# Attention keys computed fifteen heads ahead of the scores in place of twelve, with two buffers for the mean squares

## The reference

```python
q = (layernorm(x) @ Wq).reshape(B, Sq, H, D)
k = (ctx @ Wk).reshape(B, Skv, H, D)
v = (ctx @ Wv).reshape(B, Skv, H, D)
q = rmsnorm(q, gq)            # x * rsqrt(mean(x^2) + eps) * g
k = rmsnorm(k, gk)
attn = softmax(einsum('bqhd,bkhd->bhqk', q, k) / sqrt(D))
x = x + einsum('bqhk,bkhd->bqhd', attn, v).reshape(B, Sq, H * D) @ Wo
```

## Time and profile before

| | |
|---|---|
| median of 3 runs | 1373.06 us (1372.28 to 1373.51) |
| the profiled execution | 1372.17 us |
| its span, first to last instruction | 1370.4 us |
| PE busy | 1353.0 us, 99% of the span |
| PEld busy | 1214.4 us, 89% |
| DVE busy | 919.3 us, 67% |
| ACT busy | 919.9 us, 67% |
| POOL busy | 539.8 us, 39% |
| DMA | 166.36 MB, mean 121 GB/s |
| mean granted TensorE clock | 0.999 of full speed |

### The profile page before, as it was taken

One profiled execution on the slowest core, in us unless ns is written; L12 is line 12 of the kernel. 1 busy time (PEld: TensorE's weight loads), 2 busy tenths in 40 slices (PEclk: granted clock), 3 DMA queues, 4 the chain that ended last, 5 costly groups with the idle time before them and its releaser, 6 DMA issues. The chain is left out here.

```text
span 1370.4 us, 28300 instructions
## 1 busy us (share of the span) xinstructions
PE 1353.0 (99%) x9496; PEld 1214.4 (89%) x9496; DVE 919.3 (67%) x2414; ACT 919.9 (67%) x2019; POOL 539.8 (39%) x477
## 2 busy tenths in 40 slices
PE   9999999999999999999999999999999999999997
PEld 9889878999999999999999999999888888888885
DVE  6312047667777777777777777766558878887886
ACT  5566668888888878888888888787724443444342
POOL 1044326433323323323332423324824655565551
PEclk9999999999999999999999999999999999999999
DMA  8877723333444444444444444434562353334312
GB/s 248 237 197 222 207 73 95 111 104 120 126 115 130 122 123 116 141 114 115 139 117 121 132 110 129 123 92 141 159 187 62 66 111 64 71 66 113 62 32 44
DMA packets 186403, 166.36 MB, mean 121 GB/s; under 512 B 87938, under 2 KB 155540, under 8 KB 184468
## 3 DMA queue, kind: packets, MB, share of 16 engines
q1 hardware_dynamic: 178980, 151.50, 40.3%
q10 hardware_dynamic: 7280, 13.06, 3.6%
HBM read 124.57 MB, written 33.02 MB: 115 GB/s over the span
## 5 line engine op out<-in xcount | busy, mean ns | idle before, releaser
L816 POOL TENSOR_TENSOR rk_sp<-ms_sp,neg_half 124x6 f32<-124x6 f32 x128 | 170.2, 1353 | 462.7 <-DMA ms_sp<-ms 462.7
L1253 DVE CUSTOM_DVE_ANT_0 sc<-psS,rk 100x361 f32<-100x361 f32 x256 | 136.5, 533 | 131.8 <-PE psS L905 92.6
L1048 ACT ACTIVATE pr<-ex,ri 100x361 f32<-100x361 f32 x256 | 152.6, 596 | 43.4 <-DVE ri L1241 43.4
L1041 ACT ACTIVATE ex<-sc,nb,rq_all 100x361 f32<-100x361 f32 x256 | 174.8, 683 | 4.0 <-DVE nb L1262 3.9
L933 PE MATMUL psZ<-pT_hi,cK_hi 120*128 120x400 f32 (+1 forms) x384 | 132.6, 345 | 0.0
L933 PE MATMUL psZ<-pT_hi,cK_lo 120*128 120x400 f32 (+1 forms) x384 | 132.1, 344 | 0.0
L933 PE MATMUL psZ<-pT_lo,cK_hi 120*128 120x400 f32 (+1 forms) x384 | 131.9, 343 | 0.0
L918 PEld LDWEIGHTS psP<-ident,pr 100*120 100x120 f32 (+1 forms) x768 | 73.6, 138 | 42.6 <-issue 35.3
L1023 ACT ACTIVATE ring_hi<-bank 128x362 fp32r<-128x362 f32 x125 | 59.1, 473 | 75.6 <-PE bank L881 74.7
L1233 DVE TENSOR_TENSOR pT_lo<-psP,pT_hi 122x600 fp32r<-122x600 f32 x128 | 98.9, 773 | 1.2 <-ACT pT_hi L1072 1.1
L905 PE MATMUL psS<-ring_hi,q_hi 128*100 128x362 f32 x256 | 96.8, 378 | 2.0 <-DVE mx L1253 2.0
(11 more groups left out here) (324 smaller groups left out, 3895.5 us busy)
## 6 DMA issues: line engine op xcount, KB each, us to landing
rk<-rk_dram SPq DMA_DIRECT2D x128, 290.6 KB
q_dram<-q_out SPq DMA_DIRECT2D x64, 200.0 KB, 4.4
q_in<-q_dram SPq DMA_DIRECT2D x64, 200.0 KB, 3.9
o_dram<-o SPq DMA_DIRECT2D x64, 200.0 KB, 4.5
stage<-in_w_ff SPq DMA_DIRECT2D x12, 1024.0 KB, 6.5
w_in<-in_w_ff ACTq DMA_DIRECT2D x48, 256.0 KB, 4.0
o_in<-o_dram SPq DMA_DIRECT2D x12, 1024.0 KB, 6.0
cT_in<-in_ctxT SPq DMA_DIRECT2D x15, 361.0 KB, 4.2
```

The source lines that it names most:

```text
L816: nc.gpsimd.tensor_tensor(rk_sp[:, cols], ms_sp[:, cols], neg_half[0:HG * SKR, :].to_broadcast([HG * SKR, n]), op=ALU.pow).then_inc(g_rk, 1)
L1041: nc.scalar.activation(ex[:, h % 2, :], sc[:, h % 2, :], ACT.Exp, bias=nb[:, h % 2:h % 2 + 1], scale=factor(n), accum_out=rs[:, h % 2:h % ...
L1048: nc.scalar.activation(pr[:, h, SKP - SK:SKP], ex[:, h % 2, :], ACT.Copy, scale=ri[:, h % 2:h % 2 + 1]).then_inc(a_pr, 1)
L1253: nc.vector.tensor_tensor_reduce(out=sc[:, h % 2, :], in0=psS[0:SQ, 0:SK], in1=rk[:, u % 2, h, 0:SK], scale=1.0, scalar=-3.0e38, op0=ALU.m ...
```

## The change: what it does

1. LEAD goes from 12 to 15. PE, ACT and DVE start their loop at u = -4, so that fifteen keys come before score 0 (one at (-4, 1) and on), and the last key is issued at (60, 0). The keys up to number 14 use four banks.
2. The squares and mean squares of unit w stay at (w - 2, 0) and (w - 2, 1) for w from 2 on. Those of unit 0 go to (-3, 0) and (-3, 1), behind the unit's fourth key (number 3), and those of unit 1 to (-2, 0) and (-2, 1), behind key 7. Before, they stood behind keys 4 and 8.
3. `ms` gets two buffers. `mean_squares(u)` waits for the spreading DMA of unit u - 2, and `squares(u)` gets one more wait, for the mean squares of unit u - 1, since both use the bank `psNV`.
4. `high_cT` goes to (3, 2) and (4, 3) on ACT, `low_cT` to (3, 3) and (5, 0) on DVE. The first key of the even batch's next pair falls at (4, 1), that of the odd one at (5, 1); before, at (5, 0) and (6, 0).
5. SP's loop and POOL's order stay as they are (POOL's loop begins one empty unit earlier).

```diff
-    LEAD = 3 * HG
+    LEAD = 4 * HG - 1
...
-        ms = sb("ms2", [P, SKQ])
+        ms = sb("ms2", [P, 2, SKQ])
...
+        SQUARES_AT = {-3: 0, -2: 1, **{w - 2: w for w in range(2, UNITS)}}
...
-        def pipeline(eng, unit):
+        def pipeline(eng, unit, begin=-4):
...
-            for u in range(-3, UNITS + 2):
+            for u in range(begin, UNITS + 2):
...
-                sp.dma_start(ms_sp[:], ms[0:P:QW32, :].rearrange("h (i k) -> h i k", i=SKR)).then_inc(d_ms, 16)
+                sp.dma_start(ms_sp[:], ms[0:P:QW32, u % 2, :].rearrange("h (i k) -> h i k", i=SKR)).then_inc(d_ms, 16)
...
-            pipeline(sp, unit)
+            pipeline(sp, unit, -3)
...
                 pe.wait_ge(a_k, u * HG + HG)
                 if due(u - 5):
                     pe.wait_ge(a_o, u - 5)
+                if due(u):
+                    pe.wait_ge(v_ms, u)
...
-                    if h == 0 and real(u + 2, UNITS):
-                        squares(u + 2)
+                    if h == 0 and u in SQUARES_AT:
+                        squares(SQUARES_AT[u])
...
-                    if h == 0 and first in (4, 5) and real(u, UNITS) and real(b + 2, B):
-                        high_cT(b + 2)
+                    if (h, first) in ((2, 3), (3, 4)) and real(u, UNITS) and real(place(u + 1)[0] + 2, B):
+                        high_cT(place(u + 1)[0] + 2)
...
-            nc.vector.memset(ms[:, SK:SKQ], 1.0)
+            nc.vector.memset(ms[:, :, SK:SKQ], 1.0)
...
-                if due(u * 16):
-                    dve.wait_ge(d_ms, u * 16)
-                nc.vector.tensor_scalar(ms[:, 0:SK], psNV[:, 0:SK], 1.0 / D, EPS, ALU.mult, ALU.add).then_inc(v_ms, 1)
+                if due(u - 1):
+                    dve.wait_ge(d_ms, (u - 1) * 16)
+                nc.vector.tensor_scalar(ms[:, u % 2, 0:SK], psNV[:, 0:SK], 1.0 / D, EPS, ALU.mult, ALU.add).then_inc(v_ms, 1)
...
-                    if h == 1 and real(u + 2, UNITS):
-                        mean_squares(u + 2)
+                    if h == 1 and u in SQUARES_AT:
+                        mean_squares(SQUARES_AT[u])
...
-                    if h == 1 and first in (4, 5) and real(u, UNITS) and real(b + 2, B):
+                    if h == 3 and first == 3 and real(u, UNITS) and real(place(u + 1)[0] + 2, B):
+                        low_cT(place(u + 1)[0] + 2)
+                    if h == 0 and first == 5 and real(u, UNITS) and real(b + 2, B):
                         low_cT(b + 2)
```

More of the change, by code:

```diff
@@ L635, in attention @@
         p_first, v_first, g_first = s("p2_first"), s("v2_first"), s("g2_first")
-        first_st, first_mv, first_ve, first_rs = (ms[:, a:b] for a, b in ((0, 6), (6, 8), (8, 9), (9, 10)))
+        first_st, first_mv, first_ve, first_rs = (ms[:, 0, a:b] for a, b in ((0, 6), (6, 8), (8, 9), (9, 10)))
         xn0 = q_in[:].rearrange("p s n -> p (s n)")[:, 0:DIM]
```

## The result

Over 21 runs of each, the kernel before has a median of 1373.06 us (1371.68 to 1375.05) and the changed one 1375.25 us (1373.89 to 1378.03). The ratio is 1.0018, with a 95% interval of 1.0012 to 1.0024: 2.2 us more, by that interval slower, and still inside the 0.2% that counts as "the same" in the prediction. The forecast was 1375.0 us. The spans of the profiled executions, 1370.4 and 1372.7 us, differ by 2.3. The profiled execution of the kernel before, 1372.17 us, lies 0.1 us under the lowest of the three runs that the table of the time before goes by, not inside their spread as is said there; it is inside the spread of the 21.

A forecast was written before the change was run, and what follows sets the result against it. TensorE was taken to bound the kernel, leaving only start and end to move: +3.7 at the start and -1.8 at the end gave +1.9 us on 1373.06, so 1375.0 us. The range was 1372.2 to 1377.3.

The forecast's parts named there:

- What bounds the kernel: Whole kernel: TensorE is busy 99% of the span, without idle from 400 to 500 us, so only start and end can move.
- Part 1: Start: squares of units 0 and 1 right behind their fourth key make PE idle, costing 2 x 1.0 = 2.0 us.
- Part 2: Start: three more keys put score 0 at 198.7 and shift the exponential of head 4 and what follows by 3.7 us.
- This chain moves as one: Start: exponential of head 4, DVE's scaling, 1.91 us context split and waiting transpose all shift together, 3.7 us late.
- Part 3: End: three keys fewer save 3.0 us, less 1.2 for an uncovered transpose at (60, 2); gives back 1.8.
- Part 4: Added wait ahead of the squares and second mean-squares buffer: cost and gain 0; upper bound 3.2 us for the wait.
- Part 5: Moved context split: 0; the odd batch's low part in (5, 0) fits ahead of its key with 0.3 us to spare.
- DVE's wait on the broadcast: Start: sign that the case is right; DVE's 2.24 us wait for unit 0's factors should be gone.
- The long transpose: Start: sign of right, the transpose with the long wait at 216.6 us; before 215.5 would count as wrong.
- The start pays in full: Start: moved keys cover all four old waits, 3.0 - 4.0 = -1.0 us there, total 1370.3; chance 0.09.
- The end gives nothing back: End: unit 62's broadcast or later loads land late, gain lost, +3.7 us, 1376.8; chance 0.20, including start costs of 4.5 or more.
- The third wait is exposed: Added wait ahead of the squares is paid, or the context split comes late: +1.9 + 3.2, 1378.2; chance 0.06.

The follow-up runs named there:

- e1: Changed kernel with the squares of units 0 and 1 back behind their fifth key, so the three keys stand alone; ratio 1.0001 to the kernel before.
- e7: Kernel before, still twelve heads ahead, with only the squares of units 0 and 1 moved behind their fourth key; ratio 1.0005.
- e8: Kernel before with only GpSimd's order changed in unit 1, the query split behind the query factors; ratio 1.0005.
- e11: Kernel before with only the third wait ahead of the squares, mean squares still in one buffer; ratio 1.0000.
- e2: Kernel before, twelve keys ahead, with only the second mean-squares buffer and the third wait ahead of the squares; ratio 1.0007.
- e3: Changed kernel with the first batch's context split moved early, to the keys of unit -2; ratio 1.0003 to the kernel before.
- e4: Changed kernel with the value matmuls issued ahead of the transposes from unit 60 on; ratio 1.0006 to the kernel before.
- e5: Kernel before with the early context split, and values ahead of transposes from unit 60 on; ratio 0.9999.
- e10: Kernel before with the early context split and the load of the second context's keys one unit earlier; ratio 0.9986.
- e9: Changed kernel with the edits of e1, e3 and e4, plus the second context's load one unit earlier; 1371.57 us against 1373.99, ratio 0.9982.
- e12: Kernel before once more, no edit, for a second profile; a single run, 1374.16 us.

## Why the prediction was right

**What bounds the kernel**: right. From 400 to 500 us PE is busy for all 100 us in both, and nothing moved there but 0.3 us in 600.

**Part 1**, 2 x 1.0 us: right. PE idles 0.93 at each, and removing it from the changed kernel gives 2.0 (e1). The reason given, that nothing covers it, holds only with the three keys: alone, the 2.0 are gone by DVE's first scaling, and the squares of unit 4 come 0.2 later (e7).

**Part 2**: right to score 0 (198.7 forecast, 198.41 measured) and to the exponential of head 4 (+3.7 forecast, +3.65 measured from the attention's first matmul). The step that failed is the next, "This chain moves as one". The split in it was 1.91 us only because GpSimd held it up (e8); 3.7 us later it is 1.09, and the shift at the transpose is 3.1 in place of 3.7. I had taken a duration for a property of the instruction that was one of its neighbour.

**Part 3**, +1.2 - 3.0: right. The new wait is at (60, 2), of 1.06 us, and the last units give 1.7 back (forecast 1.8). Of the 1.2 charged, 0.3 had no row behind it.

**Part 4**, 0: right for the wait (e11): the separate instructions are there and are covered, and the upper bound of 3.2 us did not come about. The rule of the Trainium skill (Perfetto Trace Analysis, Identifying Dependency Chains) that such instructions may be put ahead agrees with the trace; it gives no price for them. For the second buffer, 0 is 0.34 too low by e2 against e11, and perhaps 0.3 more in the middle; together that would be most of the 0.9 that the sum lacks.

**Part 5**, 0: right within what the traces can tell. At its first use the odd batch's split ends at 258.66 us and the key starts at 259.07, 0.4 to spare (forecast 0.3). Unit 5 and those after it keep their distances.

So +1.9 came as +2.2: 3.0 - 1.7 + 0.9 in place of 3.7 - 1.8. The start was put 0.7 us too high, and 0.9 us of small items (0.4 in the middle, 0.5 behind the last squares) had no term. The terms were right in kind; that the sum came so close is partly luck, as two misses of 0.7 and 0.9 us cancelled, and the interval of the measured ratio alone is 0.8 us to either side.

Of the signs that the prediction named, the idle before the squares (0.93), score 0, DVE's wait on the broadcast (0.23 left of 2.24) and the wait at (60, 2) came as said. The long transpose came at 215.66, not at 216.6, and just above the 215.5 that was to count as wrong.

**The rivals.** *The start pays in full* fell: no wait of the start paid for the end. *The end gives nothing back* fell: the broadcast of unit 62 was issued at 963.65, its first score was scaled at 968.22, and no wait of PE hangs on it. *The third wait is exposed* fell in e11. That the start could gain if the split were moved was not among them, and it is in the fastest version. One thing stays open in part: how often the ordinary runs of the kernel before fall into the low clock at 212 us. Its two profiles do not show it; of the three variants that start like it, e2 and e11 do and e8, with the shorter wait, does not. The mean clock of each run is on record: it is 0.998, as in e11's profile (e2's fall shows as 0.999), in 11 of the 93 runs of the kernel before that stand beside the experiments, and these took 0.8 to 1.4 us longer than the others of their chip; also in 4 runs of e2, 2 of e7 and 2 of e11. In the changed kernel and in all other variants it is never that low. So it looks as if the kernel before paid now and then for its long wait and the changed one did not; where in those runs the clock fell, only the profiled ones show.

## What to carry to other kernels

A long instruction ahead of a wait should be asked why it is long: the same three subtractions took 1.1 or 1.9 us by what GpSimd did beside them, and a shift of 3 us, or another order on GpSimd, decides it. Work that is put ahead of a start shares one slack with whatever else is put there, so price such parts together and not one by one: here 0.2 and 1.0 made 3.0. And each wait taken out of a start exposes the next, here the context split, then the load behind it, then the single buffer. So e1, e3 and e4 each only brought the changed kernel back to the time before, the early split alone did nothing for the kernel before (e5), and only with the load moved as well did the time fall, by 0.14% (e10) and with all edits by 0.18% (e9).

## What the runs showed of the hardware

DVE's subtraction with both operands in SBUF took 1231 ns in place of 418 when it started 0.1 us behind a GpSimd subtraction, 794 when it started 0.54 us behind it (e7), and 1.61 us in place of 0.72 at the end of the attention (e1). Where DVE was 0.14 us ahead, GpSimd's subtraction took 1.68 us in place of 1.29 and DVE's stayed at 0.68 (e3). TensorE's granted clock fell to 0.57 over 4 us after a single idle of 1.97 and 1.94 us in e2 and e11, and stayed at 1.00 after one of 1.96 in the kernel before and of 2.17 in e12: the start of these kernels took 38.6 us without and 39.8 to 40.2 us with it, 1.2 to 1.6 us apart. In e10 it fell after 1.73. In the other nine traces, whose single waits there are 1.52 us at most, it stayed at 1.00. What decides between 1.94 with and 2.17 without a fall, no run here shows.
